# A decoder layer on one Trainium2 core: another order of work in the expert rounds, and scatters to the output that need no order among themselves

## The reference

```python
h  = LN(x + mixer(x))                    # state space scan, 16 states
h  = LN(h + cross_attention(h, [h, ctx]))  # 8 heads of 128, 256 + 77 keys
l  = softmax(h @ Wg); two experts of 8 by token, their weights normalized
y  = sum over the token's two experts of weight_e * (relu(h @ W1[e]) @ W2[e])
out = LN(h + y)
```

## Time and profile before

| | |
|---|---|
| time, median of 3 runs | 1012.4 us (1010.82 to 1012.67) |
| the profiled execution | 1019.83 us |
| its span in the trace | 1018.1 us |
| PE busy | 984.9 us (97%) |
| DVE busy | 830.5 us (82%) |
| ACT busy | 727.8 us (71%) |
| POOL busy | 580.3 us (57%) |

### The profile page before, as it was taken

The page is one execution under the profiler, slowest core; times in us unless marked ns, Lnnn a source line. Parts: engine busy times, 40 slices in busy tenths (PEclk is TensorE's granted clock), DMA queues, the critical chain, the costliest instruction groups (busy, mean ns, idle before and its releaser), DMA issues.

```text
span 1018.1 us, 21686 instructions
## 1 busy us (share of the span) xinstructions
PE 984.9 (97%) x7018; PEld 930.0 (91%) x7018; DVE 830.5 (82%) x2125; ACT 727.8 (71%) x1869; POOL 580.3 (57%) x1059
## 2 busy tenths in 40 slices
PE   8999999999999999999999999999999999999994
PEld 6789999999999999999999999999999999888783
DVE  6887878888888888888888788878887877677774
ACT  6686868787777768777878677867787766466652
POOL 4743474756566556565565557474746464436664
PEclk9999999999999999999999999999999999999997
DMA  7653031113111121104110411040204114555542
GB/s 248 199 134 112 11 114 42 54 44 104 51 51 46 68 88 51 46 24 132 51 46 16 140 51 41 7 132 29 64 27 140 47 36 148 190 178 157 166 139 70
DMA packets 63030, 88.97 MB, mean 87 GB/s; under 512 B 15540, under 2 KB 44008, under 8 KB 62920
## 3 DMA queue, kind: packets, MB, share of 16 engines
q1 hardware_dynamic: 56968, 71.10, 22.4%
q0 software_dynamic: 5952, 16.50, 4.8%
HBM read 49.31 MB, written 38.26 MB: 86 GB/s over the span
## 4 chain that ended last, share of the span: by engine, by line
PE 77%; DVE 8%; ACT 7%; issue 5%; POOL 2%; DMA 2%; another core or an unknown queue 1%; POOLq 0%; SPq 0%; DVEq 0%; ACTq 0%
PE ps L632 21%; PE ps L634 20%; PE ps L633 20%; PE ps L661 7%; PE ps L740 3%; DVE nmx L1855 2%; PE ps L676 1%; PE ps L678 1%; PE ps L778 1%; ACT hp L1097 1%; ACT prob L1254 1%; PE ps L771 1%; PE ps L764 1%; ACT ys_x L1196 1%; DMA cxs<-in_ctxt 1%
## 5 line engine op out<-in xcount | busy, mean ns | idle before, releaser
L2243 POOL TENSOR_SCALAR prob<-prob,rinv 128x333 f32<-128x333 f32 x256 | 144.0, 574 | 232.1 <-DVE rinv L1864 231.6
L632 PE MATMUL ps<-kv_lo,w_hi 128*128 128x256 f32 (+1 forms) x512 | 154.8, 302 | 1.1 <-DVE kv_lo L1413 1.1
L1249 ACT ACTIVATE oT_hi<-ps 128x256 fp32r<-128x256 f32 x126 | 48.4, 384 | 149.7 <-PE ps L678 145.7
L634 PE MATMUL ps<-kv_hi,w_hi 128*128 128x256 f32 (+1 forms) x512 | 152.9, 299 | 0.0
L633 PE MATMUL ps<-kv_hi,w_lo 128*128 128x256 f32 (+1 forms) x512 | 152.5, 298 | 0.0
L1254 ACT ACTIVATE prob<-ps,nmx 128x333 f32<-128x333 f32 x256 | 135.1, 538 | 7.7 <-DVE nmx L1855 7.7
L1413 DVE TENSOR_TENSOR pT_lo<-ps,pT_hi 128x512 fp32r<-128x512 f32 x254 | 131.0, 549 | 1.0 <-ACT pT_hi L1266 0.3
L1855 DVE TENSOR_REDUCE nmx<-ps 128x2 f32<-128x666 f32 x128 | 108.4, 847 | 8.3 <-PE ps L634 6.7
L661 PE MATMUL ps<-ident,prob 128*128 128x128 f32 (+1 forms) x768 | 106.0, 273 | 1.8 <-POOL prob L2243 1.0
L632 PEld LDWEIGHTS ps<-kv_lo,w_hi 128*128 128x128 f32 x512 | 97.0, 189 | 1.7 <-issue 1.5
L634 PEld LDWEIGHTS ps<-kv_hi,w_hi 128*128 128x128 f32 x512 | 96.8, 189 | 0.0
(11 more groups left out here) (336 smaller groups left out, 3325.5 us busy)
## 6 DMA issues: line engine op xcount, KB each, us to landing
wraw<-in_W SPq DMA_DIRECT2D x14, 512.0 KB, 4.9
vcd_hi<-vst_hi SPq DMA_DIRECT2D x10, 512.0 KB, 2.7
vcd_lo<-vst_lo SPq DMA_DIRECT2D x10, 512.0 KB, 3.7
v_hi<-vcd_hi SPq DMA_DIRECT2D x32, 154.0 KB
v_lo<-vcd_hi SPq DMA_DIRECT2D x32, 154.0 KB
slots<-initr SPq DMA_DIRECT2D x8, 522.0 KB, 9.2
xs<-in_x SPq DMA_DIRECT2D x16, 256.0 KB, 4.1
xts<-in_xT SPq DMA_DIRECT2D x15, 256.0 KB, 3.8
```

What stands on the lines that cost most here:

```text
L632: pe.matmul(dst, hi1, lo2, start=first, stop=False, skip_group_check=True)
L634: return pe.matmul(dst, hi1, hi2, start=False, stop=last, skip_group_check=True)
L2243: pool.tensor_scalar(prob[:, h % 2, t, 0:KEYS], prob[:, h % 2, t, 0:KEYS], rinv[:, h % 2, t:t + 1], 1.0, ALU.mult, ALU.mult).then_inc(norm ...
```

## The change

- `slots` rows get a sixth column, so they are 262 floats long: the number of the token's last slot (C_LAST). The initial rows are written without the token and base columns, and a new transfer writes these two columns of all 4096 slots from a tile `blank`, as 4096 pieces of 8 bytes. It stands in SP's queue between L530 and L539.
- Behind that, a slot knows whether it is its token's last one. If it is not (or is empty), `weights` adds NTOK to the row number for `out`, so its row goes to a spare row. `out` grows by the spare rows. The wait on `sc_done` in `finished` goes.
- POOL in head 7 gets one operation on 4 columns and two on 1 column. DVE's `first_slot`, one operation at two places in `ending()`, becomes `ends_of` with three. `weights` has five operations in place of three, and stands behind `sums`.
- The eps of the norm goes into the square root's bias and into one of DVE's operations, which takes one DVE operation out of each `variance`.
- DVE's and ACT's work in rounds 1 to 6 is ordered anew, and PE's `inner` waits for the first weights alone, `outer` for the second.

```diff
@@ -527,7 +530,8 @@
                 for e in range(E):
-                    sp.dma_start(slot_rows[e], initr[:]).then_inc(init_st, 16)
+                    sp.dma_start(slot_rows[e][:, :, 0:C_TOK], initr[:, :, 0:C_TOK]).then_inc(init_st, 16)
+                sp.dma_start(slots[OWN:TRASH, C_TOK:ROW].rearrange("(a p) c -> p a c", p=P), blank[:]).then_inc(init_st, 16)
 
@@ -867,6 +871,7 @@
             def outer(e, u, pairs=range(ST // 2)):
+                need(pe, wl_set, 2 * e + 2)
                 for pair in pairs:
@@ -1370,23 +1375,25 @@
                 u = e % 2
-                parts(e + 1, 1 - u)
-                relu(e, range(0, 3))
-                deviation(e - 1, e - 1, slice(0, ST))
-                relu(e, range(3, 4))
+                part1(e + 1, 1 - u)
+                relu(e, range(0, 1))
+                part2(e + 1, 1 - u)
+                relu(e, range(1, 4))
                 xparts(e + 1)
-                scale(e - 1, (0, 1), e - 1)
                 if e < E - 2:
+                    deviation(e - 1, e - 1, slice(0, ST))
                     result(e, u, (0, 1))
-                    scale(e - 1, (2, 3), e - 1)
+                    scale(e - 1, range(ST), e - 1)
                     result(e, u, (2, 3))
...
                     result_tile(e, u, 0)
+                    deviation(e - 1, e - 1, slice(0, ST))
+                    result_tile(e, u, 1)
+                    scale(e - 1, (0, 1), e - 1)
+                    result_tile(e, u, 2)
                     scale(e - 1, (2,), e - 1)
-                    result_tile(e, u, 1)
+                    result_tile(e, u, 3)
                     scale(e - 1, (3,), e - 1)
-                    for n in (2, 3):
-                        result_tile(e, u, n)
 
@@ -1648,12 +1655,16 @@
                 dve.wait_ge(step_set, 7)
-                first_slot(xrow)
-
-            def first_slot(rows):
+                ends_of(xrow, slot_b, 1)
+
+            def ends_of(rows, kept, n):
 
                 both = slot_u[:].rearrange("p (t c) -> p t c", c=2)
-                dve.tensor_tensor(rows[:, :, D + 1], both[:, :, 0], both[:, :, 1], ALU.min).then_inc(slot_set, 1)
+                dve.scalar_tensor_tensor(out=kept[:], in0=both, scalar=float(NTOK), in1=keep[:], op0=ALU.add,
+                                         op1=ALU.mult).then_inc(kept_set, 1)
+                dve.tensor_tensor(rows[:, :, C_BASE], both[:, :, 0], both[:, :, 1], ALU.min)
+                dve.wait_ge(kept_set, KEPT + n)
+                dve.tensor_tensor(rows[:, :, C_LAST], kept[:, :, 0], kept[:, :, 1], ALU.max).then_inc(slot_set, 1)
 
@@ -1889,11 +1900,15 @@
                 need(dve, xsl_ld[u], loaded)
-                dve.tensor_copy(tku[:, e], xsl[u][:, :, D:D + 2]).then_inc(cols_set, 1)
-                dve.scalar_tensor_tensor(out=wm[:], in0=xsl[u][:, :, D + 4], scalar=float(e), in1=xsl[u][:, :, D + 3],
+                dve.tensor_copy(tku[:, e, :, 1], xsl[u][:, :, C_BASE]).then_inc(cols_set, 1)
+                dve.tensor_tensor(early[:], xsl[u][:, :, C_LAST], mine[:, e], ALU.not_equal).then_inc(cols_set, 1)
+                dve.scalar_tensor_tensor(out=wm[:], in0=xsl[u][:, :, C_IDX], scalar=float(e), in1=xsl[u][:, :, C_DW],
                                          op0=ALU.is_equal, op1=ALU.mult).then_inc(cols_set, 1)
-                dve.wait_ge(cols_set, 3 * e + 2)
-                dve.tensor_tensor(wsl[:, e], wm[:], xsl[u][:, :, D + 2], ALU.add).then_inc(cols_set, 1)
+                dve.wait_ge(cols_set, COLS * e + 2)
+                dve.scalar_tensor_tensor(out=tku[:, e, :, 0], in0=early[:], scalar=float(NTOK), in1=xsl[u][:, :, C_TOK],
+                                         op0=ALU.mult, op1=ALU.add).then_inc(cols_set, 1)
+                dve.wait_ge(cols_set, COLS * e + 3)
+                dve.tensor_tensor(wsl[:, e], wm[:], xsl[u][:, :, C_W], ALU.add).then_inc(cols_set, 1)
 
@@ -1920,20 +1935,19 @@
 
-                dve.wait_ge(fstat_set, 3 * part + 1)
+                dve.wait_ge(fstat_set, 2 * part + 1)
                 for s in range(ST)[tiles]:
...
                 last.then_inc(fstat_set, 1)
-                dve.wait_ge(fstat_set, 3 * part + 2)
-                dve.tensor_scalar(f_vv[:, e, tiles], f_mv[:, e, tiles, 1], EPS, None, ALU.add).then_inc(fstat_set, 1)
-
-            def moments(e):
+
+            def moments(e, tiles):
 
                 dve.wait_ge(z_set, 2 * e + 2)
-                for s in range(ST):
+                for s in tiles:
                     last = dve.bn_stats(f_st[:, e, s, :], yo[e % 2][:, s, :])
-                last.then_inc(fstat_set, 1)
-                variance(e, e, slice(0, ST))
+                if tiles[-1] == ST - 1:
+                    last.then_inc(fstat_set, 1)
+                    variance(e, e, slice(0, ST))
 
@@ -2052,14 +2067,17 @@
                 sums(e - 1, 1)
-                moments(e - 1)
-                relu(e)
+                part1(e + 1, 1 - u)
+                relu(e, range(0, 3))
+                moments(e - 1, (0, 1))
+                relu(e, range(3, 4))
+                moments(e - 1, (2, 3))
+                xparts(e + 1)
                 shift(e - 1, e - 1, slice(0, ST))
-                xparts(e + 1)
-                parts(e + 1, 1 - u)
-                weights(e + 1, 1 - u, 16 * ((e + 1) // 2) + (16 if u == 0 else 0))
+                part2(e + 1, 1 - u)
                 if e < E - 2:
                     sums(e, 0)
+                weights(e + 1, 1 - u, 16 * ((e + 1) // 2) + (16 if u == 0 else 0))
 
@@ -2195,8 +2214,10 @@
                 pool.wait_ge(initr_set, 1)
-                pool.iota(initr[:, :, D], [[P, ST]], NTOK, 1, allow_small_or_imprecise_dtypes=True)
-                pool.iota(initr[:, :, D + 1], [[P, ST]], OWN, 1, allow_small_or_imprecise_dtypes=True).then_inc(initr_set, 1)
+                pool.iota(mine[:].rearrange("p e s -> p (e s)"), [[P, E * ST]], NTOK + OWN, 1,
+                          allow_small_or_imprecise_dtypes=True)
+                pool.iota(blank[:, :, 0], [[P, E * ST]], NTOK + OWN, 1, allow_small_or_imprecise_dtypes=True)
+                pool.iota(blank[:, :, 1], [[P, E * ST]], OWN, 1, allow_small_or_imprecise_dtypes=True).then_inc(initr_set, 1)
                 context_lo(0)
@@ -2321,8 +2342,14 @@
                         need(pool, route_step, r + 7)
+                        pool.tensor_tensor(slot_b[:], slot_a[:], keep[:], ALU.mult).then_inc(route_step, 1)
                         for t in range(NT):
-                            pool.tensor_scalar(xrow[:, t, D + 1:D + 2], slot_a[:, t, 0:1], slot_a[:, t, 1:2], None, ALU.min)
+                            pool.tensor_scalar(xrow[:, t, C_BASE:C_BASE + 1], slot_a[:, t, 0:1], slot_a[:, t, 1:2], None,
+                                               ALU.min)
+                        need(pool, route_step, r + 8)
+                        for t in range(NT):
+                            pool.tensor_scalar(xrow[:, t, C_LAST:C_LAST + 1], slot_b[:, t, 0:1], slot_b[:, t, 1:2],
+                                               float(NTOK), ALU.max, ALU.add)
                         pool.tensor_copy(slot_u[:], slot_a[:].rearrange("p t c -> p (t c)")).then_inc(slot_set, 1)
@@ -2345,7 +2372,6 @@
                     pool.wait_ge(last_st, PART + 16)
-                need(pool, sc_done, 64 * B + 64 * e)
                 for n in tiles:
```

More of the change, by code:

```diff
@@ L43 @@
 REST = CTX - 32
-STEPS = 11
+STEPS = 12
 KROWS = [P, P, CTX + REST]
@@ L47 @@
 CT = -(-B * CTX // P)
-ROW = D + 5
+ROW = D + 6
 OWN = NT * P
@@ L52 @@
 QSCALE = float(DH) ** -0.5
+C_W, C_DW, C_IDX, C_LAST, C_TOK, C_BASE = range(D, D + 6)
 S0, T0, AVB, WOB, G0, NG = 0, 2, 3, 4, 5, 3
@@ L109, in build @@
         ident = sb("ident", [P, P])
-        powm = sb("powm", [P, 4])
+        powm = sb("powm", [P, 5])
+        eps1 = powm[:, 4:5]
         warm = sb("warm", [P, 4])
+        mine = sb("mine", [P, E, ST])
         rawbuf = ExitStack()
@@ L158, in build @@
         initr = sb("initr", [P, ST, ROW], F32, clear)
+        blank = sb("blank", [P, E * ST, 2], F32, clear)
         clear.close()
@@ L182, in build @@
         oT_lo = s1("oT_lo", [P, 2, S], F32R)
-        nmx = s1("nmx", [P, 2, NT])
-        rsum = s1("rsum", [P, 2, NT])
-        rinv = s1("rinv", [P, 2, NT])
+        sums3 = s1("sums3", [P, 3, 2, NT])
+        nmx, rsum, rinv = [sums3[:, i] for i in range(3)]
         e1 = s1("e1", [NST, S])
@@ L204, in build @@
         x_st = s1("x_st", [P, 6])
-        x_mv = s1("x_mv", [P, 2])
-        x_vv = s1("x_vv", [P, 1])
-        x_rs = s1("x_rs", [P, 1])
+        x_cols = s1("x_cols", [P, 4])
+        x_mv, x_vv, x_rs = x_cols[:, 0:2], x_cols[:, 2:3], x_cols[:, 3:4]
         cfull = s1("cfull", [P, KD, P])
@@ L228, in build @@
         dd, w2u, den, gate = [pairs[:, i, :] for i in range(4)]
-        wgt = s1("wgt", [P, NT, 2])
+        routed = s1("routed", [P, 5, NT, 2])
+        wgt, rank, keep, slot_a, slot_b = [routed[:, i] for i in range(5)]
         tot = s1("tot", [P, NT, E], F32R)
```

(21 more changed lines are left out.)

39 lines of the change are left out of this document (17 added, 22 removed).

## The result

The changed kernel takes 1016.53 us (median of 6 runs, 1015.78 to 1017.96), the kernel before in the same comparison 1012.27 us (1010.82 to 1013.42, 6 runs). The ratio is 1.0046, with a 95% interval of 1.0036 to 1.0056: the change makes this kernel slower, by 4.3 us. The forecast was 1014.0, in a range of 1009.2 to 1019.5.

A forecast was written before the change was run, and what follows sets the result against it. PE was taken to bound the kernel, with 77% of the chain. +3.3 + 0.4 − 0.8 − 1.3 = +1.6 gave 1021.4 us profiled, 1014.0 for the median; own range 1012 to 1016.5, wider 1009.2 to 1019.5.

The forecast's parts named there:

- The `blank` transfer: At the start, 4096 small pieces ahead of `xts` in SP's queue make PE stall at L734: +3.3 us.
- the bounds of 1.6 to 5.9: PE's stall for `xts` at the start: 1.6 us at least by the issue, 5.9 us by the queue.
- Both pictures of mine: At the start, pieces priced by SP's issue (stall 1.6 to 4.1 us) or by the queue (stall 5.9 us).
- the issue's bound: SP's issue goes by pieces: 4096 take 10.1 to 12.6 us, `xts` lands 3.8 us after its issue.
- PE's clock should stay: Behind the stall for `xts`, PE's granted clock stays at 1.00, as after an earlier 2.50 us; no cost added.
- a rival, for a stall of 12 us: At the start, pieces at 3.1 ns behind the whole queue stall PE 12 us, plus 1.6 for clock: 1024.3; chance 0.13.
- The attention loop, 0 forecast for POOL: POOL's added head 7 operations, 0.85 us 15 times, stay hidden under 4.8 us of cover: 0.
- The end of the last batch: `ends_of` adds two operations behind L1687, where PE waits for `bh_lo`, and 0.1 elsewhere: +0.4 us.
- The rounds: In the middle expert rounds, the new order removes about a third of 2.2 us of PE's waits: −0.8 us.
- The end, −1.3: At the last scatters, `finished(7)` begins at 1009.5 rather than 1010.88 without the wait on earlier scatters: −1.3 us.
- sign of being wrong: The prediction is wrong if PE waits for `prob` in the attention loop, or its waits in the rounds grow in sum.
- The first rival: At the start, the pieces pass beside the rest without a stall: −2.1 us, 1010.3, faster; chance 0.26.

The follow-up runs named there:

- `with_wait`: The changed kernel with the wait on all earlier scatters put back into `finished`; 1032.11 us, 1.0074 of the kernel before.
- `before_again`: The kernel before itself, unchanged, run and profiled once more; 1011.58 us, ratio 0.9991.
- `after_again`: The changed kernel itself, run again on another chip; 1013.10 us, 1.0011 of the kernel before.
- `before_place`: The kernel before, no instruction changed, with unused `mine` and merged small tiles giving the changed kernel's tile places for the attention loop; 1012.46 us, 1.0007 of the kernel before.
- `old_order_2`: The changed kernel with the old order of DVE, ACT and PE's weight waits in rounds 1 to 6; 1013.41 us, 1.0013 of the kernel before.
- `late_2`: The changed kernel with the 8-byte pieces issued behind the first batches' loads, second run; 1011.76 us, 0.9997 of the kernel before.
- `late_mine_end`: The changed kernel with the pieces issued behind the first loads and tile `mine` moved behind the large tiles; 1011.01 us, 0.9993 of the kernel before.
- the first group: The first four follow-up kernels, run on one chip where the kernel before took 1023.9 us; their ratios to it were 1.0028 to 1.0083.
- `before_blank`: The kernel before with the same 4096 8-byte pieces at the same queue place, written to an unused table; 1028.78 us, 1.0049 of the kernel before.
- `old_order`: The changed kernel with the old order of DVE, ACT and PE's weight waits in rounds 1 to 6, first run; 1032.48 us, 1.0083 of the kernel before.
- `late`: The changed kernel with the 8-byte pieces issued behind the first batches' loads, first run; 1027.16 us, 1.0028 of the kernel before.

## Why the prediction was right or wrong

**The `blank` transfer, +3.3 forecast: right place, too small.** The wait stood at L738 (L734 of before), for the landing of `xts`, and was 3.99 us long, within the bounds of 1.6 to 5.9. In other executions with the same pieces ahead of `xts` it was 3.34, 2.15, 1.85, 1.40 and 0.79 us (the row of the 1.85, in `with_wait`, names DVE, but the wait ends with the landing of `xts` at 68.02), so this term, the largest, differs by 3 us from one execution to the next. As far as one trace of each can tell, that is also why the change costs 4.3 us in the first comparison and 1.1 in the second: the first `seen` comes at 148.5 and at 145.3. Both pictures of mine were half right: SP did stand for some 9.6 us, as the issue's bound had it, but in the row of the next transfer, and `xts` then needed 5.2 us more, not 3.8. The landing moved by 5.3 us for 4096 pieces, 1.3 ns each, and by 4.7 from `before_again` to `after_again`, 1.1 ns each: under the 1.6 that rows 7 gave as the most.

**"PE's clock should stay": wrong, and it cost 1.6 us.** I concluded from a wait of 2.50 us without effect to one of 3.3. After 2.15 us the clock indeed stayed at 1.00, after 3.34 and 3.99 it was 0.50. I had the half clock in a rival, for a stall of 12 us, with the right price; it belonged in the main sum. So the start was 5.8 us: 142.1 to 148.5 is 6.4, of which 0.6 lay before the transfer (64.46 against 63.84 for the last work ahead of the wait).

**The attention loop, 0 forecast for POOL: right for POOL, and yet 1.3 us lost.** The sum had no term for it: it costed every instruction and left out that the change moves tiles. `before_place` has about 1.2 us of this loss.

**The end of the last batch, +0.4: half of it.** From the fifteenth `seen` to the first matmul of the last batch's expert layer it is 18.6 us in `before_again` (874.8 to 893.41) and 18.85 in `after_again` (879.6 to 898.45), +0.2.

**The rounds, −0.8: nothing.** The waits of rows 15 were of that one execution; `before_again` has none of them. I had taken only a third of them, but carried every term over to the median by subtracting 7.4 us, as if that surplus lay elsewhere; it lay in the expert rounds: from the first matmul of the last batch's expert layer to PE's last one it is 110.8 us in that trace and 101.3 in `before_again`. Between the new order and the old (`old_order_2`) 0.3 us lie in the medians, less than can be told. A wait of 0.9 us at the last expert (L2075), which stood in the first trace too and which I hadn't costed, went with the places of the tiles: `before_place` is without it, and the old order doesn't bring it back.

**The end, −1.3: right,** 1.71 to 0.37 us.

The sum is then 5.6 + 1.3 + 0.2 + 0 − 0.9 − 1.3 = +4.9, against 4.3 measured, in which the 5.6 is that of the one profiled execution. The forecast's +1.6 lacked the clock (1.6), the tiles (1.3), 0.7 of the wait, and the 0.8 that the rounds didn't give, and had 0.9 of gain too little and 0.2 too much for the last batch. It was right about where the change loses and gains, at the start and at the end. The total lies 2.5 us above the forecast, at the upper edge of its own range of 1012 to 1016.5 (the wider one reaches to 1019.5), and by the measure of 0.2% the answer is slower, to which I had given 0.36, and not same (0.38). Neither sign of being wrong showed: PE didn't wait for `prob` in the loop, and its waits in the rounds fell.

The first rival (pieces pass beside the rest) was put at 1010.3, with −1.2 for the rounds where the sum has −0.8; with −0.8 it is 1010.7. `late_2` and `late_mine_end`, in which the pieces don't stand ahead of `xts`, are 0.3 and 0.7 us under before. The long stall of 12 us was off: even 8192 pieces gave 5.91 us of wait. The Trainium skill, in DMA: Bandwidth & Descriptors, under Bandwidth, gives about 10.5 ns for a packet, from a load of 64 packets; an estimate from that figure is 43 us for 4096. The first pair of traces has 1.3 ns a piece. (With 43 us in front of `xts` the stall would have been 42.4 and the sum 39 us worse, not the 35 that I wrote.)

**What stays open.** On the chip of the first group the loop took 739.0, 738.1 and 738.5 us in the three kernels with the changed code, and 733.2 in `before_blank`. Whether the same cause as in `before_place` is at work, 4 to 5 times as strong, was not tried. Nor which of the merged or moved tiles it is, and why a place should cost time. What makes the stall for `xts` 0.8 us in one execution and 4.0 in another isn't known either. On that chip `old_order` had 7.3 us of PE's waits for `h_lo`, `with_wait` 3.2, `late` 4.6 and `before_blank` 4.1:

```profile
PE ps L636 <- DVE h_lo L1852: 7.3, 4, 3.0
```

Each is one execution, so whether the new order helps where the signals come late stays open too.

## What to carry to other kernels

A transfer is priced by its pieces and by what stands behind it in its queue: 32 KB in 8-byte pieces, ahead of a load with 0.6 us of slack, cost more in the first comparison than all else that the change did. If PE is to wait for more than it has been seen to wait without a fall of its clock, add the fall. And a wait that appears in a profiled execution far above the median is no gain to be had until a second profile shows it.

## What the runs showed of the hardware

A loop in which PE is busy for 298.9 of 300 us took 1.2 us longer (733.0 to 734.2) when only tiles moved by 32 to 128 bytes and some small ones were put side by side; no single wait shows it, and a wait of 0.9 us elsewhere went with it. Behind `xts` a granted clock of 0.50 followed idle times of 3.34 us and more, and 1.00 those of 2.15 us and less; but in the first trace of before 0.51 followed a row of waits near 991 to 995 us of which none is over 1.0 us. The same 4096 pieces ahead of the same load made PE wait 0.8 to 4.0 us. An issue of 4096 pieces took SP 1.37 us, and the next issue 9.56 (6.46 to 9.89 in other executions): the price of a transfer can stand in the row of its successor.
